# Route stage of a graph, mixing and expert kernel: four products of the identity behind each tile's transposes

## The reference

```python
xn = _layernorm(x)
x = x + graph_attention(xn, src, dst) + mix(xn)          # one row of 256 per node
x = x + ffn(_layernorm(x))

def mix(x):      # linear attention over all nodes, so one 256 x 256 matrix serves all of them
    q, k, v = split(x @ W_qkv + b_qkv)
    ...
    kv = einsum('bnc,bnd->bcd', k2, v)
    t2 = einsum('bnc,bcd->bnd', q2, kv) / sqrt(N)
    return (v + t2) @ W_out + b_out

def ffn(x):      # 8 experts, the two best for each node
    probs = softmax(x @ router_w.T)
    topk_probs, topk_idx = top_k(probs, 2)
    ...
    h = silu(x @ w1[e]) * (x @ w3[e]);  y = h @ w2[e]
    return sum of gates * y
```

## Time and profile before

| what | us |
|---|---|
| median of three runs | 2865.88 (2858.85 to 2868.88) |
| the profiled execution, and its span | 2872.26, 2870.5 |
| route stage in the profile, from its first matmul to the first expert matmul | 1793.85 to 2039.57 |
| TensorE busy, share of the span | 2320.9, 81% |
| VectorE busy | 1806.3, 63% |
| ScalarE, GpSimd busy | 1253.3, 44%; 1144.3, 40% |
| mean clock granted to TensorE | 0.842 of 2.4 GHz |

### The profile page before, as it was taken

One profiled execution on the slowest core, in us unless ns is written; L12 is line 12 of the kernel. 1 busy time (PEld: TensorE's weight loads), 2 busy tenths in 40 slices (PEclk: granted clock), 3 DMA queues, 4 the chain that ended last, 5 costly groups with the idle time before them and its releaser, 6 DMA issues.

```text
span 2870.5 us, 47292 instructions
## 1 busy us (share of the span) xinstructions
PE 2320.9 (81%) x12659; PEld 1906.3 (66%) x12683; DVE 1806.3 (63%) x6119; ACT 1253.3 (44%) x3758; POOL 1144.3 (40%) x1155
## 2 busy tenths in 40 slices
PE   3999984777877787778777878754599999999998
PEld 1677653555655565556555656643599999999997
DVE  8667763776777767777776667645355555555553
ACT  7444424555555555555555555432122222222222
POOL 0000005666666666666666663245222112112211
PEclk9999985788778777887788787765799999999999
DMA  2233213333333333333333335654122222222222
GB/s 71 92 115 99 90 59 85 88 89 89 89 89 89 89 89 89 89 88 89 90 89 89 89 88 52 213 179 157 52 36 36 34 36 35 36 34 36 36 35 28
DMA packets 127236, 226.62 MB, mean 79 GB/s; under 512 B 25553, under 2 KB 86482, under 8 KB 126214
## 3 DMA queue, kind: packets, MB, share of 16 engines
q0 software_dynamic: 62448, 142.98, 21.5%
q1 hardware_dynamic: 64534, 80.65, 9.0%
HBM read 169.81 MB, written 53.72 MB: 78 GB/s over the span
## 4 chain that ended last, share of the span: by engine, by line
PE 46%; DVE 18%; issue 16%; another core or an unknown queue 9%; DVEq 5%; POOL 2%; ACT 1%; DMA 1%; POOLq 0%; SPq 0%; ACTq 0%
PE psum L1614 18%; PE psum L1647 9%; PE psum L1102 6%; DVEq L1221 4%; DVE arena L1202 3%; PE psum L495 2%; DVE arena L824 2%; DVE arena L825 2%; DVE arena L1213 2%; PE psum L1353 1%; DVE arena L1246 1%; POOL expert_in L1574 1%; DVEq L1202 1%; PE psum L502 1%
## 5 line engine op out<-in xcount | busy, mean ns | idle before, releaser
L1075 POOL DMA_INDIRECT arena<-table,arena x880 | 864.2, 982 | 496.1 <-issue 235.9
L1102 PE MATMUL psum<-arena 128*128 128x257 f32 x1760 | 707.4, 540 | 293.6 <-DVE arena L1202 220.6
L1102 PEld LDWEIGHTS psum<-arena 128*128 128x128 f32 x1760 | 385.5, 255 | 509.3 <-issue 414.4
L1202 DVE SCALAR_TENSOR_TENSOR arena<-arena,psum 128x257 f32 x880 | 423.3, 481 | 358.8 <-remote 284.7
L1614 PE MATMUL psum<-arena 128*128 128x128 f32 x4620 | 552.1, 275 | 0.6 <-ACT arena L1669 0.6
L1614 PEld LDWEIGHTS psum<-arena 128*128 128x128 f32 x4620 | 542.5, 192 | 6.7 <-DVE arena L1711 0.9
L1751 POOL DMA_INDIRECT out<-arena x105 | 163.2, 1555 | 674.7 <-ACT arena L1676 664.6
L1129 ACT ACTIVATE arena<-arena 128x128 f32<-128x128 bf16 x880 | 281.2, 391 | 148.6 <-DVE arena L1216 108.4
L1647 PE MATMUL psum<-arena 128*128 x1260 | 290.5, 379 | 0.8 <-ACT arena L1676 0.8
L1142 ACT ACTIVATE arena<-arena 128x128 f32<-128x128 bf16 x880 | 281.2, 391 | 7.8 <-PE psum L1102 0.7
L1093 PEld LDWEIGHTS psum<-arena 128*128 128x128 f32 x1760 | 251.2, 220 | 19.1 <-issue 18.9
(11 more groups left out here) (332 smaller groups left out, 3093.1 us busy)
## 6 DMA issues: line engine op xcount, KB each, us to landing
arena<-table,arena POOLq DMA_INDIRECT x880
arena<-expert_in SPq DMA_DIRECT2D x105, 129.0 KB
mix_inputs<-arena SPq DMA_DIRECT2D x98, 128.0 KB
arena<-mix_inputs SPq DMA_DIRECT2D x49, 256.0 KB
arena<-in_w SPq DMA_DIRECT2D x6, 1364.0 KB
out<-arena SPq DMA_DIRECT2D x50, 128.0 KB
table<-arena SPq DMA_DIRECT2D x49, 129.0 KB
arena<-in_x SPq DMA_DIRECT2D x49, 128.0 KB, 3.6
```

Source lines behind the costliest of these rows:

```text
L1075: pool.indirect_dma_start(rows_in[j][:, q * TW:(q + 1) * TW], None, table_d[:, :], bass.IndirectOffsetOnAxis(ap=col_all[:, t:t + 1], axis=0))\
L1102: mm(psum[4 + q][:, 0:C + 1], weight[b][:, q * P:(q + 1) * P], rows_in[g][:, q * TW:q * TW + C + 1], start=True, stop=True).then_inc(S("pr ...
L1202: v.scalar_tensor_tensor(here, here, alpha[(j - 5) % RING][:, q:q + 1], psum[4 + q][:, 0:C + 1], ALU.mult, ALU.add).then_inc(S("acc_done"), 1)
```

## The change

Behind `turn(i - 4)` in each of the 49 steps that have a `mix(i)`, TensorE multiplies the identity by itself four times, into columns 128 to 255 of PSUM bank 7, which nobody reads. No semaphore is waited for or raised by these products. The four calls of a step are eight MATMUL records with eight weight loads. In the first four steps there is no `turn` yet, and they stand directly behind `mix(i)`. In steps with `offsets` they stand ahead of it.

```diff
 SLOPE = 0.01
+IDLE_ROUTE = 4
 EPS = 1e-5
...
                 if 0 <= i - 4 < NT:
                     turn(i - 4)
+                if i < NT:
+                    for _ in range(IDLE_ROUTE):
+                        mm(psum[7][:, P:2 * P], ident[:, :], ident[:, :], start=True, stop=True)
                 b = batch_of(i, RB + 6)
                 if b is not None:
                     offsets(b)
```

## The result

The changed kernel takes 2879.87 us, the median of four runs (2878.80 to 2883.94). The kernel before, run beside it on the same chip, takes 2863.07 (2858.85 to 2868.88). The ratio is 1.006, with a 95% interval of 1.0037 to 1.0082: slower by 0.6%, some 17 us. The forecast was 2889, with a range of 2863 to 2920. The changed kernel's profiled execution took 2883.94 us (span 2882.2, clock 0.849), 11.7 us more than the profiled one of before.

The account below looks back on a forecast made before the run. The route stage's end was taken to hang on when GpSimd's last train of 34 sends starts. Terms 6 + 15 + 2 = +23 us on the profiled 2872.3 gave 2895, or 2889 against the median; range 2863 to 2920.

Parts of the forecast that it names:

- the tail: Route stage, steps 49 and later: no products there, covered by 44 us of GpSimd's sends, so no cost.
- The tile: One route-stage step with four products: 2.49 us at full clock (1.59 before), 4.58 at the half (2.88 before).
- The opening: Route stage until the first burst of GpSimd's sends, 14 steps: terms +3.4, +3.9 and a 1.2 gain, sum +6 us.
- A period: Seven tiles with a 14-send burst: the stretch behind the burst grows from 11.40 to 15.2 us, +3.8, four times: +15.
- The ration counts instructions: During sends only 91 TensorE instructions pass in 20.10 us: 2.5 tiles, not 4.5, so two fall behind the burst.
- Rival 1: Products lie in idle time, including 7.5 us per burst when all but GpSimd stand still: no change, 2866; chance 0.19.
- The first interval: Route stage, first burst, of seven sends, half a full one: +2 us.
- The clock: Route stage: after a standstill one tile at half clock, the rest full; whole stage up from 0.61 to some 0.75.
- Rival 2: Clock returns to full at once behind each burst's standstill, no half-clock tile: gain of 10 us, 2856; chance 0.09.
- The bounds: Products rationed in full, one or two more half-clock tiles behind each burst: +7 or +8 us there, some +38 whole.
- Rival 3: Clock stays down, all five tiles behind a burst take 4.58 us: 2926; chance 0.14 including mixtures toward it.

Follow-up runs that it names:

- the wide product: One 512-column product a step in place of the changed kernel's four of 128: 2614.55 us, ratio 1.0025 to the kernel before; again 2616.49, ratio 1.0027.
- the narrow products: Four products of 8 columns a step in place of the changed kernel's 128 columns: 2702.98 us, ratio 1.0364 to the kernel before.

## Why the prediction was right, and where it wasn't

**Bound and direction: right.** The stage's end hangs on the start of the last train (34 sends, 43.8 us, as forecast), the tail costs nothing, and the added work on TensorE delays the train. Both intervals, on the first chip and on the others, lie above 1.

**The tile: right, with one slip.** The half-clock tile measured 4.62 (4.58 forecast). At the full clock it measured 2.38 in the opening, not 2.49. The forecast added 0.90 to 1.59, but the 1.59 was VectorE's pace. TensorE's own was 1.48, so only 0.79 of the 0.90 came onto the path.

**The opening: mis-sized.** Forecast +6, measured +2.3 from the stage's first matmul. (By the absolute times the first burst is 3.18 us later, just over the bound of 3 that the prediction had set.) The trace splits it. The sets of steps 0 to 3 were forecast at +3.4 and brought +1.5 at the first transpose, since one of them ran at the half clock and not two, and `mix(1)` behind the first ran at the full clock already (1.03 us at 1798.24). The set of step 4, which the forecast left out, brought +0.9. Steps 5 to 11 were forecast at +3.9 and brought +1.2: here is the step that failed. It priced them all at the full clock and took off the 2.41 us wait, but `mix(11)`, right behind the wait, was at the half clock already (2.07 us in the earlier trace rows), so that `mix(5)` to `mix(12)` took 15.5 us in the kernel before and not the 13.5 of the forecast; the slip of the tile makes up the rest. Steps 12 to 14 gave back the 1.2 us that were forecast. On the chips without late completions the opening cost +5.9. That this meets the forecast's 6 is luck: the first burst of the changed kernel comes at +41.9 and +41.7 on the two, but that of the kernel before at +39.6 and +35.8, since there `mix(10)` to `mix(13)` take 4.8 us and not 10.1, with no wait for a load between them.

**A period: mis-sized, and its step failed.** Forecast +3.8, measured 7.2 / 4 = +1.8. "The ration counts instructions" is the step: 131 instructions passed in 20.10 us where 91 had. A tile there grew from 20.10 / 4.55 = 4.42 us to 20.10 / 3.64 = 5.52, by 1.1 us, which is near the 0.90 us that its products take at the full clock. So 0.9 of a tile fell out of the burst, not 2, and the stretch behind it took 13.33 us, not 15.2 (11.40 before). Whether the late completions charge a TensorE instruction anything beyond its own time was to be told by the wide product, and stays open. Rival 1, under which the products would lie in the idle 7.5 us for nothing, is ruled out too: it needed 4.5 tiles in a burst, where 3.6 passed, and periods 1.2 us shorter, where they are 1.8 longer.

**The first interval**: +0.8, forecast +2, the same step at half size.

**The clock: right in kind, low in size.** One tile at the half behind a halt, the rest full, as in the rows from 1883.03 on; 0.79 to 0.87 over the bursts' periods, against a forecast of 0.75. Rival 2 needed 1.00 right behind the halt, and the row of 1883.03 is at the half. Even where nothing halts and the clock never falls, the products cost 9 us, since the clock was not what the stage lacked.

**The sum**: 6 + 2 + 15 = 23 was forecast, 2.3 + 0.8 + 7.2 = 10.3 came in the trace. So the terms together were more than twice too large. That the medians came out at +17, near the 23, owes 5 us to differences between executions that neither trace explains: the direction and the path were foreseen, the closeness of the number is in part luck.

**Slips in the working.** The bounds put a period at +7 or +8 for one or two more tiles at the half clock; 3.8 and 2.09 or 4.18 are 5.9 and 8.0. Rival 3 kept the opening at +6, though a clock that stays down costs far more there: the narrow products, where it did, had their first burst 31 us later.

## What to carry to other kernels

Products that are to keep TensorE's clock up are paid for at their full time once they outrun the slack to the engine that paces the loop; find that slack first. Here it was 0.1 us a tile to VectorE, with 17.9 us of sends per seven tiles as a second cover: two products made the period 18.7 us, at no cost that the runs could tell, four made it 20.3. The fillers with few columns were the worst choice: they took nearly the time of wide ones, and the clock stayed at 0.50. A price must be taken from the engine's own pace, not from the loop's, and two kernels are to be compared on the same chip.

## What the runs showed of the hardware

- TensorE can be busy 99.8% of 227 us and be granted 0.50 all the while, when much of that is weight loads for eight-column float32 calls. The same number of calls with 128 columns held 1.00.
- The same kernel takes 2608 us on some chips and 2863 on others. On the latter TensorE's completions reach their consumers up to 13.6 us late while GpSimd issues indirect transfers, and fewer such transfers among the tiles (7 in place of 14 a batch) brought the longest down to 5.0 us. VectorE's and ScalarE's signals are on time in the same traces.
- A float32 call of 128 columns costs 0.22 us at the full clock, by the tiles of kernels with two, four and eight of them.
